# Turning the attention matrix in 32 by 32 squares: a macaron transformer block in split float32 on one Trainium2 core

## The reference

```python
x = x + 0.5 * ffn(layernorm(x))      # 256 -> 1024, exact gelu, -> 256
x = x + attn(layernorm(x))           # 16 heads of 64, ALiBi slopes, causal
x = x + 0.5 * ffn(layernorm(x))      # same weights
# attn, per head h:
sim  = (q * 64**-0.5) @ k.T - slope[h] * abs(i - j)
sim  = where(j > i, -max, sim)
out  = softmax(sim) @ v              # then @ w_out + b_out
```

## Time and profile before

| | |
|---|---|
| median of 3 runs | 2598.97 us (2595.24 to 2600.84) |
| the profiled execution, its own time | 2596.59 us |
| its span, first to last instruction | 2594.8 us |
| mean granted TensorE clock | 0.987 of full |
| PE, DVE, ACT, POOL busy | 96%, 61%, 47%, 27% of the span |

### The profile page before, as it was taken

How to read it: one execution, slowest core, us unless ns; L and a number is a source line. 1 busy time by engine, 2 the same in 40 slices (tenths; PEclk the granted TensorE clock), 3 DMA queues, 4 the chain that set the end, 5 groups by cost and what they waited for, 6 DMA issues and landing times.

```text
span 2594.8 us, 44129 instructions
## 1 busy us (share of the span) xinstructions
PE 2490.0 (96%) x16256; PEld 1946.8 (75%) x16256; DVE 1591.5 (61%) x4454; ACT 1219.0 (47%) x3032; POOL 696.5 (27%) x1130
## 2 busy tenths in 40 slices
PE   7999999999999999999999999999999999999997
PEld 5777687777868778687786877768777687776876
DVE  6665656656566566666656566665655656656554
ACT  5535535354353544536445263553635536355352
POOL 2313223232231322313223132231412313123231
PEclk9999999999999999999999999999999999999998
DMA  3000000000000000000000000000000000000000
GB/s 118 1 1 17 1 17 1 1 18 1 17 1 1 17 1 17 1 1 17 1 17 1 1 17 1 17 1 11 7 1 17 1 17 1 1 17 1 9 1 9
DMA packets 21876, 26.16 MB, mean 10 GB/s; under 512 B 1696, under 2 KB 20384, under 8 KB 21664
## 3 DMA queue, kind: packets, MB, share of 16 engines
q1 hardware_dynamic: 21664, 23.34, 2.9%
HBM read 14.95 MB, written 8.39 MB: 9 GB/s over the span
## 4 chain that ended last, share of the span: by engine, by line
PE 88%; DVE 7%; ACT 3%; issue 1%; DMA 0%; POOL 0%; SPq 0%; DVEq 0%
PE psR L246 64%; PE psS L246 12%; PE psR L367 11%; DVE gl L600 3%; ACT P L517 2%; DVE xtl L600 1%; DVE gh L650 1%; PE psR L285 1%; ACT gt L502 1%; DVE ol L600 1%; DVE xn L623 0%; ACT xth L494 0%; DVE wql L725 0%; DMA raw<-in_L_ffn_w 0%; DVE x L629 0%
## 5 line engine op out<-in xcount | busy, mean ns | idle before, releaser
L825 POOL TENSOR_SCALAR P<-P,rs 128x512 f32<-128x512 f32 (+3 forms) x1024 | 526.3, 533 | 1071.4 <-DVE rs L662 1071.4
L517 ACT ACTIVATE P<-P,mx 128x512 f32<-128x512 f32 (+3 forms) x1024 | 562.0, 552 | 189.1 <-DVE mx L672 189.1
L672 DVE CUSTOM_DVE_ANT_0 P<-psS,dist 128x512 f32<-128x512 f32 (+3 forms) x1024 | 441.3, 487 | 289.8 <-PE psS L246 289.8
L682 DVE COPY PT<-psR 128x512 f32<-128x512 f32 x640 | 408.8, 678 | 31.2 <-PE psR L367 30.7
L367 PE MATMUL psR<-ident,P 128*128 128x128 f32 x2560 | 328.9, 276 | 30.7 <-DVE xtl L600 30.3
L367 PEld LDWEIGHTS psR<-ident,P 128*128 128x128 f32 x2560 | 285.3, 141 | 84.5 <-DVE xtl L600 33.9
L246 PE MATMUL psS<-qk 64*128 64x512 f32 (+3 forms) x2048 | 345.9, 455 | 0.7 <-ACT qk L482 0.7
L246 PE MATMUL psR<-PT,v 128*64 128x512 f32 (+3 forms) x2048 | 321.8, 459 | 0.0
L246 PE MATMUL psR<-w2h,gh 128*128 128x256 f32 x1024 | 296.5, 290 | 5.9 <-DVE gl L600 5.9
L246 PEld LDWEIGHTS psS<-qk 64*128 64x128 f32 x2048 | 176.6, 186 | 158.1 <-issue 117.1
L246 PE MATMUL psR<-w2l,gh 128*128 128x256 f32 x1024 | 289.5, 283 | 0.0
(11 more groups left out here) (66 smaller groups left out, 4487.3 us busy)
## 6 DMA issues: line engine op xcount, KB each, us to landing
x<-in_L_attn_x SPq DMA_DIRECT2D x16, 512.0 KB, 4.7
out_y<-x SPq DMA_DIRECT2D x16, 512.0 KB, 3.2
raw<-in_L_ffn_w SPq DMA_DIRECT2D x2, 512.0 KB, 5.7
raw<-in_L_ffn_w SPq DMA_DIRECT2D x1, 1024.0 KB, 8.6
rawq<-in_L_attn_w_qkv SPq DMA_DIRECT2D x1, 1024.0 KB, 7.2
rawk<-in_L_attn_w_qkv SPq DMA_DIRECT2D x1, 1024.0 KB, 9.3
rawv<-in_L_attn_w_qkv SPq DMA_DIRECT2D x1, 1024.0 KB, 6.3
rawo<-in_L_attn_w_out SPq DMA_DIRECT2D x1, 1024.0 KB, 5.5
```

The costliest lines, as they stand in the source:

```text
L517: e.activation(p, p, ACT.Exp, bias=mx[:, r, i:i + 1], scale=-1.0, accum_out=sm[:, r, i:i + 1]).then_inc(s_ex.sem, 1)
L672: e.tensor_tensor_reduce(out=P[c % 2][:, h, cs], in0=score_block(h, i), in1=dist[:, T - w:T], scale=-SLOPE[2 * c + h], scalar=BIG, op0=ALU ...
L682: e.tensor_copy(PT[c % 2][:, heads, col:col + w], src).then_inc(s_tc.sem, 1)
L825: e.tensor_scalar(p, p, rs[:, 2 * (c % 2) + h, i:i + 1], 1.0, ALU.mult, ALU.mult).then_inc(s_nz.sem, 1)
```

## The change

P is no longer transposed by PE. Its columns are laid out as four groups m of 32-column squares, so that one DVE transpose, in place, turns every 32 by 32 square of a half of P (`HALF`: 4 x 448 columns with blocks 3 and 2 of both heads, then 4 x 192 with blocks 0 and 1). SP then moves partition group g of column group m to partition group m of PT, sixteen DMAs of 32 partitions by 640 elements (80 KB) a pair (`spread`). `values` reads PT in runs of 32 elements, in twelve matmuls a pair instead of eight. P gets three buffers. All eight score blocks of a pair are computed in one burst into six banks, and during pairs 0 to 6 everything else shares banks 6 and 7; outside, the ring has all eight. The order of the streams around it changes too: v tiles move (two in turns 0 and 1, none in turn 2), all `up` tiles stand before `values` of pair 7, `dn` of tile 2 moves into turn 0, ACT copies the v tile before the exps of block 1, DVE does both reciprocals and then, at the head of the next turn, the statistics (at c = 5) and the transpose; the residual stream has two buffers instead of three. The wait of the v copy quoted above is not touched. `inverse`, `stats`, `proj_copy` and the other helpers keep their work.

```diff
-    QBASE = {3: 0, 2: 512, 0: 896, 1: 1024}
-    KBASE = {0: 0, 1: 512, 3: 896, 2: 1024}
     QORDER = (3, 2, 0, 1)
-    PW = 1280
-    TURNS = ("both j2", "even j13", "even j0", "odd j13", "odd j0")
+    GW = 640
+    HALF = {1: slice(0, 448), 0: slice(448, GW)}
+    RUNS = ((0, (0, 1)), (0, (2, 3)), (1, (1, 2)), (1, (3,)), (2, (2, 3)), (3, (3,)))
+
+    def block_at(h, i):
+
+        return 224 * h + 96 * (i - 2) if i >= 2 else 448 + 96 * h + 32 * i
...
-    x0 = place("x0", [128, NT, D], F32)
-    x1 = place("x1", [128, NT, D], F32)
-    x2 = place("x2", [128, NT, D], F32)
+    xb = [place(f"x{i}", [128, NT, D], F32) for i in range(2)]
...
-    P = [place(f"P{i}", [128, 2, PW], F32, PP + 8 * PW * i) for i in range(2)]
-    PT = [place(f"PT{i}", [128, 2, PW], F32, PT_AT + 8 * PW * i) for i in range(2)]
-    gt = place("gt", [128, 3, T], F32, GT)
-
-    g_at = {1: [SPARE, QK, QK + 4096, V, PP, PP + 4096, V + 4096, PT_AT + 16384],
-            2: [PT_AT + 4096 * m for m in range(5)] + [SPARE, V + 4096, PP + 10240]}
+    P = [place(f"P{i}", [128, 4, GW], F32, PP + 16 * GW * i) for i in range(3)]
+    PT = [place(f"PT{i}", [128, 4, GW], F32, PT_AT + 16 * GW * i) for i in range(2)]
+    gt = [place(f"gt{i}", [128, T], F32, a) for i, a in enumerate((GT, GT + 2048, PP + 28672))]
...
-    psS = nc.alloc_psum_tensor("psS", [128, 4 * 512], F32)
-    psR = nc.alloc_psum_tensor("psR", [128, 4 * 512], F32)
+    ps = nc.alloc_psum_tensor("ps", [128, 8 * 512], F32)
     def score_block(h, i):
-        bank = (h, 0) if i in (3, 1) else (2 + h, 384 if i == 0 else 0)
-        at_col = 512 * bank[0] + bank[1]
-        return psS[:, at_col:at_col + 128 * (i + 1)]
-
-    ring = []
+        at_col = 512 * (h + {3: 0, 2: 2, 0: 2, 1: 4}[i]) + (384 if i == 0 else 0)
+        return ps[:, at_col:at_col + 128 * (i + 1)]
...
     def v_tiles(c):
-        if c < 6:
-            return [("v", c // 2, c % 2)]
-        return [("v", 3, 0), ("v", 3, 1)] if c == 6 else []
+        return {0: [("v", 0, 0), ("v", 0, 1)], 1: [("v", 1, 0), ("v", 1, 1)], 3: [("v", 2, 0)], 4: [("v", 2, 1)],
+                5: [("v", 3, 0)], 6: [("v", 3, 1)]}.get(c, [])
...
+    s_pt = [Signal(f"spread{i}", [(b, c) for b, c in pairs if c % 3 == i], 16 * 16) for i in range(3)]
...
+            def spread(b, c):
+
+                if c >= 2:
+                    e.wait_ge(s_pv.sem, s_pv.at((b, c - 2)))
+                elif c == 0 and b > 0:
+                    e.wait_ge(s_dn.sem, s_dn.at((2, b - 1, NT - 1)))
+                e.wait_ge(s_tr.sem, s_tr.at((b, c, 0)))
+                for m in range(4):
+                    for g in range(4):
+                        e.dma_start(PT[c % 2][32 * m:32 * m + 32, g, :],
+                                    P[c % 3][32 * g:32 * g + 32, m, :]).then_inc(s_pt[c % 3].sem, 16)
+
             for b in B:
-                if b + 1 < NB:
-                    load_x(b + 1)
-                store_y(b)
+                for c in range(NC):
+                    spread(b, c)
+                    if c == 1 and b > 0:
+                        store_y(b - 1)
+                    if c == 2 and b + 1 < NB:
+                        load_x(b + 1)
+            store_y(NB - 1)
...
+                n = turn[0]
+                while True:
+                    n = (n + 1) % 8
+                    if n in among[0]:
+                        break
+                turn[0] = n
+                bank_free(n)
+                held[n] = use
+                bank_number[use] = n
...
-            def scores(b, c, blocks):
-                n = pairs.index((b, c))
+            def scores(b, c):
                 e.wait_ge(s_pc.sem, s_pc.at((b, ("q", c))))
-                for i in blocks:
+                for i in QORDER:
                     w = 128 * (i + 1)
                     for h in range(2):
...
+                        if i != 0:
+                            bank_free(h + {3: 0, 2: 2, 1: 4}[i])
+                            held[h + {3: 0, 2: 2, 1: 4}[i]] = ("scores", b, c, 0 if i == 2 else i, h)
                         hs = slice(64 * h, 64 * h + 64)
-                        mm(score_block(h, i), qk[c % 2][hs, 0, i * 128:i * 128 + 128], qk[c % 2][hs, 1, 0:w],
+                        keys = qk[c % 2][hs, 1, 0:w].rearrange("p (j m s) -> p m j s", m=4, s=32)
+                        mm(score_block(h, i), qk[c % 2][hs, 0, i * 128:i * 128 + 128], keys,
                            True, True).then_inc(s_qk.sem, 1)
-
-            def turn(b, c, part):
...
             def values(b, c):
                 pv = bank_for(("values", b, c))
                 e.wait_ge(s_pc.sem, s_pc.at((b, ("v", c // 2, 1))))
-                e.wait_ge(s_tc.sem, s_tc.at((b, c, TURNS[-1])))
...
+                e.wait_ge(s_pt[c % 3].sem, s_pt[c % 3].at((b, c)))
+                for n, (j, blocks) in enumerate(RUNS):
+                    i = blocks[0]
+                    for h in range(2):
+                        p = PT[c % 2][:, 0, block_at(h, i) + 32 * j]
+                        step = block_at(h, blocks[-1]) - block_at(h, i)
+                        turned = AP(p.tensor, p.offset, [[4 * GW, 128], [step, len(blocks)], [GW, 4], [1, 32]])
+                        last = mm(pv[64 * h:64 * h + 64, 128 * i:128 * i + 128 * len(blocks)],
+                                  v[(c // 2) % 2][:, j, 2 * (c % 2) + h, :], turned, n == 0, n == len(RUNS) - 1)
                 last.then_inc(s_pv.sem, 1)
...
             def attention(b):
                 more = b + 1 < NB
                 for c in range(NC + 2):
                     if c < NC:
-                        scores(b, c, (3, 2, 0))
+                        scores(b, c)
+                    if c == 0:
+                        among[0] = (6, 7)
+                    if c == NC - 1:
+                        among[0] = range(8)
+                    if c == 0 and b > 0:
+                        dn(2, b - 1, 2)
+                    if c + 1 < NC:
+                        proj_tile(b, ("k", c + 1))
                     if c == 0 and b > 0:
                         dn(2, b - 1, 3)
-                    if c + 1 < NC:
-                        proj_tile(b, ("k", c + 1))
                     if more and c == NC - 1:
                         ln_transpose(1, b + 1, 0)
-                    if c < NC:
-                        scores(b, c, (1,))
-                    if more and c == NC - 1:
                         ln_transpose(1, b + 1, 1)
                     if more and c == NC:
-                        up(1, b + 1, [2])
-                    if 1 <= c <= NC:
-                        for part in TURNS[:2]:
-                            turn(b, c - 1, part)
+                        up(1, b + 1, [2, 3, 4])
+                    if more and c == NC + 1:
+                        up(1, b + 1, [5, 6, 7])
                     if c + 1 < NC:
                         proj_tile(b, ("q", c + 1))
-                    if 1 <= c <= NC:
-                        for part in TURNS[2:]:
-                            turn(b, c - 1, part)
                     for tile in v_tiles(c):
                         proj_tile(b, tile)
-                    if more and c == NC:
-                        up(1, b + 1, [3])
-                    if more and c == NC + 1:
-                        up(1, b + 1, [4, 5])
                     if c >= 2:
                         values(b, c - 2)
...
-                if more:
-                    up(1, b + 1, range(EARLY, NM))
...
             def attention(b):
                 more = b + 1 < NB
                 for c in range(NC + 3):
+                    if more and c == NC:
+                        gelu(1, b + 1, [0, 1])
                     if c >= 3:
                         out_copy(b, c - 3)
+                    if more and c == NC:
+                        gelu(1, b + 1, [2, 3, 4])
+                    if more and c == NC + 1:
+                        gelu(1, b + 1, [5, 6, 7])
                     if c < NC:
-                        if more and c == NC - 1:
-                            ln_hi(1, b + 1, 0)
                         exps(b, c, 3)
                         if c + 1 < NC:
                             proj_copy(b, ("k", c + 1))
                         if more and c == NC - 1:
+                            ln_hi(1, b + 1, 0)
                             ln_hi(1, b + 1, 1)
                         exps(b, c, 2)
                         if c + 1 < NC:
                             proj_copy(b, ("q", c + 1))
                         exps(b, c, 0)
-                        exps(b, c, 1)
                         for tile in v_tiles(c):
                             proj_copy(b, tile)
-                    if more and c == NC:
-                        gelu(1, b + 1, range(4))
-                    if more and c == NC + 1:
-                        gelu(1, b + 1, [4, 5])
+                        exps(b, c, 1)
...
             def biased(b, c, i):
-                w = 128 * (i + 1)
-                cs = slice(QBASE[i], QBASE[i] + w)
```

(53 more changed lines are left out.)

184 lines of the change are left out of this document (62 added, 122 removed).

## The result

The changed kernel takes 2718.73 us (median of 4 runs, 2709.65 to 2725.76) against 2597.10 us for the kernel before on the same chip (2595.00 to 2600.84): a ratio of 1.0465, interval 1.043 to 1.050. It is 122 us slower. The forecast was 2614 us, slower with a chance of 0.58, range 2480 to 2820: the sign and the range held, the point was 105 us too low. The profiled execution took 2720.84 us, its span 2719.0 us.

A forecast was written before the change was run, and what follows sets the result against it. PE was taken to bound the kernel before, the ring beside it after. A middle sequence, 76.6 + 38.5 us, costs +0.8, times 15 +12; the last +3.5; from 2596.6 to 2612, median 2614 us; range 2480 to 2820.

The forecast's parts named there:

- the term of the queue: SP's sixteen issues a pair: 0.46 us each, 7.4 us a pair, PT ready 9.3 us after the short transpose.
- The third rival: SP's issues set the pace above 0.65 us each; 2820 us at 0.75; sign SP busy without gaps; chance 0.11.
- PE's work and the turns: Attention, turns 0 to 6: PE spared 15 us, 10 lost again; sum 76.6 us against 81.7.
- the ring: `biased`, exps, `inverse`, normalise and long transpose on DVE, ACT, POOL: 9.0 us a turn beside PE's 9.15.
- the waits for the k and q copies: PE in full turns: v tile waits for the k copy (a + 2.8), values for the q copy (a + 4.5).
- the kept wait of the v copies: Turns 3 and 5: ACT's v copy waits for an earlier pair's values; in turn 3, a is 3.8, not 2.1.
- The first rival: PE sets the pace of full turns, 9.2 us each: 2378 us, half of that gain 2490; chance 0.22.
- The transposes: DVE's two transposes a pair, 1,792 and 768 elements a partition: 1.95 and 0.88 us.
- The second rival: DVE transposes take twice as long, making the ring 11.7 us: 2940 us; chance 0.13.
- the reckoning with the 311 ns: DVE transposes priced by the skill's 311 ns per 128 by 128: 6.2 us a pair, near 3050 us.
- Values in runs of 32 elements: PE's twelve value matmuls reading PT in 32-element runs: no extra cost, bounds nothing to 0.5 us a turn.
- The end and the clock: Pair 7's scores to `out_proj`: two PE waits over 3 us, half clock behind each; 38.5 us against 32.6.

The follow-up runs named there:

- the third experiment: The changed kernel with sixteen transfers a pair of 128 partitions by 160 elements, P copied but not moved between partition groups: 2724.78 us, ratio 1.0492.

## Why the prediction was right in sign, in part by luck, and 105 us off

**The step that failed is the term of the queue**: "Back to back they start 0.43 us apart and one lasts up to 0.51 us; I take 0.46, 7.4 us a pair", and from it "So PT is ready 9.3 us after the short transpose". Measured were 0.63 us and 10.0 to 10.4 us a pair, and PT is ready 12.7 us after the short transpose (mean of the 128 pairs). The value came from two issues, a store and a load, and the earlier trace rows held half a hint: the store, first in the queue, took 0.39 us, the load behind it 0.51. With the 0.04 between them the price of an issue behind another would have been 0.55 us, 8.8 us a pair, still too low: these rows have no copy from SBUF to SBUF. In the kernel after, an issue after a pause takes 0.51 us and each that follows 0.59, with 0.04 between them.

Put the runs in order of the time from the end of the short transpose to the landing of the last part of PT (mean over the 128 pairs, from the landings in the traces), and the time follows:

| PT filled by | ready after us | sequence us | time us |
|---|---|---|---|
| one issue | 6.3 | 153.9 | 2518 |
| eight issues | 8.2 | 157.5 | 2568 |
| twelve on SP, four on ACT | 9.8 | 159.2 | 2593 |
| sixteen issues, half the bytes from pair 2 on | 12.6 | 165.4 | 2705 |
| sixteen issues (the kernel after) | 12.7 | 166.9 | 2719 |
| sixteen issues of 128 partitions | 12.9 | 167.1 | 2725 |
| by HBM | 14.2 | 172.7 | 2816 |

At the forecast's 9.3 us the table gives some 2585 us, an estimate between its second and third row. So the queue was worth 134 us more than the prediction had it (2719 less 2585), and all its other terms together were 29 us too dear (2614 less 2585): 105.

**The sign was in part luck.** The kernel nearest to what the prediction assumed of the queue is the one with twelve issues on SP (7.6 us a pair, PT ready after 9.8). It took 2593 us, 0.16% less than the kernel before (0.06 to 0.25%). Had the term of the queue been right, the time would have been that of the kernel before within 0.3%, and "slower" would not have come true. The other terms were too dear, this one far too cheap, and so the sign came out.

**How the 3.4 us act.** Two ways. In turns 1 to 3 the queue sets the pace: the short transposes of pairs 0 to 2 end 9.9 and 9.4 us apart in the mean, SP needs 10 to 11 us for each pair, and starts pair 2's transfers 2.4 us late in the mean; turn 2 lasts 11.3 us in the mean against 8.8 with one transfer. Then the turns are longer and the queue is on time again (late by 0.2 to 0.5 us), but its length still lies open at the end, where each PT is waited for. Turn 5 loses as well, 12.8 us in the mean against 11.1: the values of pair 3 run at a mean clock of 0.85 there, and PE waits 2.6 us for copies of ACT, not 1.6; why these come later was not settled. In the middle sequence shown, from pair 7's scores, the short transpose ends at 21.7 us (forecast 19.0; with one transfer 19.6), the last issue at 31.8, values begin at 33.4 (forecast 28.4), and `out_proj` at 40.3. Against one transfer a sequence loses 4.2 us in the turns and 8.4 at the end.

**The third rival is what happened, at its own threshold.** It said that the queue decides above 0.65 us a transfer and gave 2820 us at 0.75. The mean stretch of sixteen issues is 10.44 us, 0.65 each. Its sign, SP busy without gaps, came in half: SP still waited before 64 pairs. What was missing in it was the ground between: I had it as a cliff, but each us of readiness costs 16 to 26 us up to 9.8 us, 43 from there to 12.7, and 65 beyond. What I brought for it, the 32 partitions, had no part in it, as the third experiment shows. The Trainium skill (DMA: Bandwidth & Descriptors, anatomy of one DMA) gives a fixed 2.0 us, for a DMA that GpSimd issues. The 80 KB that SP issues here land in 2.1 us, which agrees with the size of it. The landings overlap, 2.1 us long and 0.63 apart, and only the issues add up.

**PE's work and the turns: right.** With the queue out of the way turns 0 to 6 of a middle sequence last 13.95, 9.88, 8.81, 10.62, 10.64, 11.08 and 10.63 us, 75.6, where the forecast had 14.1, 10.0, 9.2, 10.7, 10.65, 11.35 and 10.65, 76.6. So the ring, the waits for the k and q copies and the kept wait of the v copies were sized well: of the 15 us that PE is spared in these turns 6 stay (81.7 less 75.6; forecast 5). The kept wait of the v copies is part of what is lost: with v later and one transfer 48 us came back, 3 a sequence. The sign forecast for it came too: in the middle sequence with one transfer ACT sits idle 1.8 us before the copies of v tiles (2, 0) and (3, 0), until values are done. The first rival, PE sets the pace, is out: with the queue out of the way turns 3, 4 and 6 still last 10.6 us, and with eight issues, and with twelve and four, they do too.

**The transposes: right.** The two forms in the kernel after (busy us, mean ns | idle before):

```profile
L674 DVE STREAM_TRANSPOSE P<-P 128x1792 f32<-128x1792 f32 x128 | 259.3, 2025 | 9.2 <-POOL P L812 9.2
L674 DVE STREAM_TRANSPOSE P<-P 128x768 f32<-128x768 f32 x128 | 124.5, 972 | 0.0
```

2.03 and 0.97 us against 1.95 and 0.88: the price of `biased` an element carried over to the transpose. The second rival, at 3.9 us, is out. So is the reckoning with the 311 ns that the Trainium skill gives (VectorE: DVE Perf Modes, the three transpose paths): that figure is for 128 by 128 in bf16, and the twenty float32 blocks of a pair took 3.0 us in two instructions, 0.15 each, not 6.2.

**Values in runs of 32 elements: right.** 24 matmuls in place of 16, and still 2.31 us (1081.75 to 1084.06), as in the earlier trace rows.

**The end and the clock: right in kind, short in number.** The two waits of over 3 us with half clock behind each came as said. What the prediction did not have is the waits before the values of pairs 5 and 6 (2.7 and 1.5 us in the mean), with a lower clock behind them as well. With one transfer PE does not wait before these two at all, all values run at full clock, and only the wait before `out_proj` (3.13 us) and its clock stay.

The forecast's 38.5 us had the clock's loss in `out_proj` in it. Measured are 39.8 us to the start of `out_proj` (32.3 in the kernel before, mean of 15 sequences), and 1.8 us more behind it (47.68, against 159.63 - 78.59 - 32.26 - 2.9 = 45.88 before). Together with the turns (79.4 in the mean, forecast 76.6) a sequence takes 7.2 us more than before, where the forecast had 0.8: 96 us in 15 sequences. The last sequence takes 114.4 us from its first scores to `out_proj` (79.2 and 35.2), where the forecast had 103.6: 11 us more.

## What to carry to other kernels

Price a DMA that is split into many by what an issue costs behind other issues on that engine, times their number, and add one landing: here 0.63 us each for copies from SBUF to SBUF, whatever the bytes, and 0.47 for reads of HBM. Read that price from a run of issues of the same kind and not from a pair of them. In a kernel that computes the reference, a second engine's queue is what helped here (126 us). Eight transfers and one gained more, but leave out the move between partition groups, and the detour that keeps it with five issues lost 97 us. A latency that the middle of a stage hides lies open at its end, where a clock that falls in the wait adds to it.

## What the runs showed of the hardware

- Behind another one, an issue of a copy from SBUF to SBUF takes the queue of SP or ACT 0.59 to 0.61 us, 0.63 to 0.64 start to start, the same for 40, 80 and 160 KB and for 32, 64 and 128 partitions; after a pause it takes 0.46 to 0.51. Of the 2,048 in the kernel after, 48 took over 1 us; why was not settled.
- Reads of HBM, 320 KB each, take 0.43 us behind one another, and 0.30 after a pause.
- The store of `x`, 512 KB, is issued in 0.39 us when first in the queue, in 0.58 us right behind copies from SBUF to SBUF, as the timeline of SP in the kernel after shows, and in 0.43 us behind reads of HBM (median of 14 in the detour over HBM). So the same transfer has three prices, and what stands ahead of it in the queue decides. By what means was not settled.

```profile
1090.33 0.58 SPq L215 DMA_DIRECT2D out_y<-x  x1
1091.02 11.19 SPq L241 DMA_DIRECT2D PT<-P  x16
```

- 1,280 KB from SBUF to SBUF in one transfer land 6.1 us after the issue. Counted from the short transpose, they are there after 6.3 us, in 8 transfers after 8.2 us, in 16 after 12.7 (waits for the queue included).
- In the kernel after two waits of PE of 1.2 and 2.1 us, close together, were followed by a granted clock of 0.50, and one of 2.25 us by 0.70 in the mean over 3.3 us, where a wait of 1.84 us in the kernel before was followed by full matmul durations.
